# Attention scores from scaled float16 halves instead of rounded float32 halves, and a last period written out with ten products moved into the tail

## The chip, the cores and the metric

The kernel runs on one core of one Trainium2 chip. The metric is the device time of one execution in microseconds. Engine names are the profile's: PE is TensorE's matmul side and PEld its weight loads, DVE is VectorE, ACT is ScalarE, POOL is GpSimd, SP is SyncE, which only issues DMAs here. A kernel is measured several times; one of its executions is also profiled. About 0.3% (2 us) is what such a measurement can tell from no change.

## What is computed

One post-norm transformer layer on x of 4 batches x 512 tokens x 512 features, all float32. Attention has 16 query heads of 32 features and one key and value head for all of them, with rotary embedding. The feed-forward part has 1408 hidden features, with weights rounded to -1, 0, 1.

```python
q = rotary((x @ Wq + bq) as 16 heads);  k = rotary(x @ Wk + bk);  v = x @ Wv + bv
attn = softmax(q @ k.T / sqrt(32));     x = layernorm(x + (attn @ v) @ Wo + bo)
w = clip(round(w / (mean|w| + 1e-8)), -1, 1)          # for w1, w2, w3
x = layernorm(x + (sigmoid(x @ w1.T) * (x @ w2.T)) @ w3.T)
```

## The kernel before

**Periods.** The work is written out by hand for each engine, and semaphores tie the engines together. Period b (b = 0 to 3) does attention for batch b, and beside it the feed-forward part of batch b-1. Period 0 has no feed-forward work; it loads and rounds the three feed-forward weights instead (`abs_sum` on ACT, `thresholds` on DVE, `round_weight` on POOL). Periods 1 to 3 are one hardware loop, `Fori(1, B)`. A tail does the feed-forward part of batch 3 alone.

**Opening of a period.** PE projects the first four heads (q0) and k and v, multiplies the context of the batch before with Wo (`project_out`, tiles wo0 to wo3), and transposes the normed rows (`turn_h`, ht0 to ht3). DVE rotates q0 and k (`pairs`, `rotate`, `halves`), adds the residual (`attended`), computes statistics, norms, and does `h_low`. The first product of the feed-forward part, `up` of tile 0, waits for the `h_low` of ht3.

**Sixteen heads.** A head h has four score products (128 queries x 512 keys each). For each, DVE takes the row maximum (`row_max`, L702; q carries a minus sign, so it is a minimum), ACT computes the exponential with that value as bias (`exps`, L478) and sums the row, PE transposes the result (`turn`, L953), and ACT and DVE share the copies out of PSUM (`move`, L486 and L709). After each fourth head the context product follows (`context`, L1006). The list `BESIDE` says which other work stands beside head h: the up products of tile 0 to 10, the projections q2 and q3 at heads 4 and 8, and the down products dn0 to dn3 at heads 13 to 16. In period 0 q2 and q3 are projected in pieces at heads 2, 3 and 6, 7 and `halves` of q3 runs at head 9. The score tiles are a ring of three PSUM banks (four in period 0), so that a score waits for the exponential of three (four) scores before.

**Split of q and k.** The scores need more than half precision. `halves` writes the rotated q into `hi` as float32r (a rounded float32) and the remainder into `lo`; k goes to `k_st` in the same way. SP then stacks `hi`, `lo`, `hi`, `lo` of each head under each other in `q_st` with 16 small DMAs for four heads (`stack`, L283, 64 KB each, 32 partitions), and k_st holds k's parts to match, so that one product over 128 rows gives the sum of the cross products. The scale 1/sqrt(32) is put in with q's bias (L445).

**SP's order in period 0.** x transposed (`xT_sb`, two halves), the rest of Wq, the first half of w1, stack q0, rest of w1, w2, stack q1, Wo, stack q2, w3, stack q3, x into `xb` (L326), then `load_xT(1)` (L289), the next batch's transposed x. In periods 1 and 2 the next `load_xT` also stands behind stack q3.

**The tail.** PE: four `project_out`, four `turn_h`, eleven times two up tiles, four down tiles. They use the two banks `a_ps` and `b_ps` in turn. DVE norms and does `h_low` between them.

## Time and profile before

| what | us |
|---|---|
| median of 3 runs | 682.1 (681.53 to 683.32) |
| the profiled execution | 681.93, of which the traced span is 680.1 |
| PE busy in the span | 632.1 (93%) |
| DVE busy | 465.1 (68%) |
| ACT busy | 352.9 (52%) |
| POOL busy | 133.8 (20%) |

The four periods and the tail start at 0, 131.9, 286.2, 441.5 and 595.3 us on PE. Busy shares are means over stages with different limits, so that the question for each edit is which wait ends last at its place. Matmuls overlap, and a matmul's own length is longer than its share of PE's time: eight float16 products in a row last 1.90 us by their own ends, and 1.74 us from the first start to the start of what follows.

### The profile page before, as it was taken

How to read it: one execution, taken by the hardware profiler on the slowest of the kernel's cores; microseconds unless marked ns; L12 is line 12 of the kernel's file. 1: busy time of each engine (PE TensorE's matmuls, PEld its weight loads, DVE VectorE, ACT ScalarE, POOL GpSimd, SP SyncE). 2: the span in 40 equal slices, each digit the busy share in tenths (PEclk: the TensorE clock that was granted, in tenths of full speed). 3: DMA queues.
4: the chain of work that ended last, by engine and by line, in shares of the span. 5: the costliest groups of instructions: out<-in, count | busy, mean ns of one | idle time of the engine just before them, and what ended most of it. 6: DMA issues, size and time to landing. Idle time of an engine off the chain costs nothing.

```text
span 680.1 us, 10942 instructions
## 1 busy us (share of the span) xinstructions
PE 632.1 (93%) x3342; PEld 344.0 (51%) x3342; DVE 465.1 (68%) x795; ACT 352.9 (52%) x814; POOL 133.8 (20%) x148
## 2 busy tenths in 40 slices
PE   6787867899999999999999999999999999988996
PEld 2553544445656556435656555544656565543442
DVE  1767687377878976568877985567878985563333
ACT  1686696315757675114757674214757674302320
POOL 0309779231001200121000400022000400020001
PEclk9689989899999999999999999999999999998999
DMA  7670623020420220020320220020221100000001
GB/s 271 203 237 21 212 68 121 0 63 1 124 51 13 59 66 1 36 82 12 95 70 25 49 77 1 35 75 20 69 86 35 41 23 1 32 31 1 0 1 62
DMA packets 20515, 42.02 MB, mean 62 GB/s; under 512 B 4704, under 2 KB 5856, under 8 KB 19936
## 3 DMA queue, kind: packets, MB, share of 16 engines
q1 hardware_dynamic: 19488, 39.86, 19.2%
q10 hardware_dynamic: 960, 1.33, 0.5%
q8 instruction: 34, 0.56, 0.3%
q14 instruction: 33, 0.27, 0.1%
HBM read 20.20 MB, written 4.19 MB: 36 GB/s over the span
## 4 chain that ended last, share of the span: by engine, by line
PE 73%; DVE 10%; issue 7%; ACT 4%; DMA 3%; SPq 1%; POOL 1%; DVEq 0%; POOLq 0%; ACTq 0%
PE t_ps L953 14%; PE a_ps L913 11%; PE b_ps L913 11%; PE c_ps L1006 8%; PE a_ps L879 7%; PE s_ps L942 6%; PE a_ps L928 6%; PE b_ps L928 6%; DMA late<-in_w 2%; DVE sh_sb L702 2%; PE a_ps L900 2%; ACT p_sb L478 2%; SPq L283 1%; DVE stat L669 1%; PE b_ps L900 1%
## 5 line engine op out<-in xcount | busy, mean ns | idle before, releaser
L478 ACT ACTIVATE p_sb<-s_ps,sh_sb 128x512 f32<-128x512 f32 x240 | 164.2, 688 | 85.6 <-DVE sh_sb L702 85.6
L702 DVE TENSOR_REDUCE sh_sb<-s_ps 128x1 f32<-128x512 f32 x240 | 157.8, 681 | 1.5 <-PE s_ps L942 1.4
L953 PE MATMUL t_ps<-table_sb,p_sb 128*128 128x128 f32 x1024 | 140.4, 281 | 16.2 <-ACT pt_sb L486 13.9
L953 PEld LDWEIGHTS t_ps<-table_sb,p_sb 128*128 128x128 f32 x1024 | 120.6, 144 | 56.0 <-ACT p_sb L478 21.2
L709 DVE COPY pt_sb<-t_ps 128x512 f32<-128x512 f32 x128 | 88.3, 690 | 82.6 <-PE t_ps L953 80.3
L486 ACT ACTIVATE pt_sb<-t_ps 128x512 f32<-128x512 f32 x128 | 76.4, 597 | 58.1 <-PE t_ps L953 56.3
L942 PE MATMUL s_ps<-k_st,q_st 128*128 128x512 f32 x240 | 90.6, 460 | 3.7 <-DVE k_st L629 2.5
L913 PE MATMUL a_ps<-late,q 128*128 128x512 f16 x352 | 85.0, 386 | 3.5 <-DVE late L644 3.4
L913 PE MATMUL b_ps<-late,q 128*128 128x512 f16 x352 | 83.7, 381 | 0.0
L358 POOL TENSOR_TENSOR rot<-raw,table_sb 128x512 f32<-128x512 f32 x20 | 25.8, 1288 | 246.4 <-ACT raw L445 231.5
L879 PE MATMUL a_ps<-xT_sb,wq_sb 128*128 128x512 f32 x128 | 63.1, 625 | 7.9 <-DMA wq_sb<-in_wq 6.4
L382 POOL TENSOR_SCALAR rstd<-mv 128x1 f32<-128x1 f32 x32 | 8.4, 263 | 279.0 <-DVE mv L672 278.9
L1006 PE MATMUL c_ps<-pt_sb,v_sb 128*32 128x512 f32 x512 | 58.2, 595 | 0.4 <-DVE pt_sb L709 0.4
L913 PEld LDWEIGHTS a_ps<-late,q 128*128 128x128 f16 x352 | 32.0, 99 | 46.8 <-issue 7.9
L913 PEld LDWEIGHTS b_ps<-late,q 128*128 128x128 f16 x352 | 31.9, 98 | 39.5 <-issue 5.6
L942 PEld LDWEIGHTS s_ps<-k_st,q_st 128*128 128x128 f32 x240 | 42.6, 197 | 12.4 <-ACT p_sb L478 6.2
L478 ACT ACTIVATION_READ_ACCUMULATOR p_sb<-s_ps,sh_sb 128x1 f32 x240 | 48.1, 201 | 0.0
L900 PE MATMUL a_ps<-wo_sb,cx 128*128 128x512 f32 x88 | 40.2, 600 | 1.4 <-DVE late L692 1.4
L928 PE MATMUL b_ps<-q,late 128*128 128x512 f16 x176 | 41.4, 380 | 0.0
L928 PE MATMUL a_ps<-q,late 128*128 128x512 f16 x176 | 40.4, 380 | 0.0
L879 PEld LDWEIGHTS a_ps<-xT_sb,wq_sb 128*128 128x128 f32 x128 | 23.7, 198 | 32.8 <-issue 23.5
L659 DVE SCALAR_TENSOR_TENSOR b_ps<-th,b_ps 128x512 f32<-128x512 f32 x33 | 23.0, 696 | 21.5 <-PE b_ps L913 19.4
(80 smaller groups left out, 614.1 us busy)
## 6 DMA issues: line engine op xcount, KB each, us to landing
q_st<-hi SPq DMA_DIRECT2D x128, 64.0 KB, 2.0
q_st<-lo SPq DMA_DIRECT2D x128, 64.0 KB, 2.0
late<-in_w SPq DMA_DIRECT2D x2, 2816.0 KB, 11.7
xT_sb<-in_xT SPq DMA_DIRECT2D x8, 512.0 KB, 4.7
late<-in_x SPq DMA_DIRECT2D x4, 1024.0 KB, 5.6
out<-late SPq DMA_DIRECT2D x16, 256.0 KB, 2.0
late<-in_w SPq DMA_DIRECT2D x2, 1408.0 KB, 7.0
wo_sb<-in_wo SPq DMA_DIRECT2D x1, 1024.0 KB, 5.4
```

The source lines that it names most:

```text
L358: pool.tensor_tensor(rot[:, 0, :], raw[:, u % 2, :], cos_sb, ALU.mult).then_inc(cos_done, 1)
L478: act.activation(p_sb[:, h % 2, t, :], score_bank(b, n), ACT.Exp, bias=sh_sb[:, n % (2 * SR):n % (2 * SR) + 1], scale=-1.0, accum_out=sums ...
L486: act.activation(pt_sb[:, h % PTR, k, :], t_ps[k % 2][:, :], ACT.Copy).then_inc(pt_act, 1)
L702: dve.tensor_reduce(sh_sb[:, n % (2 * SR):n % (2 * SR) + 1], score_bank(b, n), AX.X, ALU.min).then_inc(maxed, 1)
L709: dve.tensor_copy(pt_sb[:, h % PTR, k, :], t_ps[k % 2][:, :]).then_inc(pt_dve, 1)
L879: mm = pe.matmul(a_ps[:, :], wq_sb[:, k, g * P:(g + 1) * P], xT_sb[:, k, :], start=(k == 0), stop=(k == DT - 1))
L900: mm = pe.matmul(ps[:, :], cx[:, g, t * P:(t + 1) * P], wo_sb[:, g, :], start=(g == 0), stop=(g == HG - 1))
L913: mm = pe.matmul(ps[:, :], w[:, k, f * P:(f + 1) * P], hT[:, s, k, :], start=(k == 0 and s == 0), stop=(k == DT - 1 and s == 1))
L928: mm = pe.matmul(ps[:, :], gT[:, s, f, t * P:(t + 1) * P], q3v[:, f, :], start=(f == 0 and s == 0), stop=(f == FT - 1 and s == 1))
L942: pe.matmul(score_bank(b, n), q_st[:, h % (QR * HPG), t * P:(t + 1) * P], k_st[:, :], start=True, stop=True).then_inc(scored, 1)
L953: mm = pe.transpose(t_ps[k % 2][:, t * P:(t + 1) * P], p_sb[:, h % 2, t, k * P:(k + 1) * P], id_sb)
L1006: mm = pe.matmul(c_ps[HD * j:HD * (j + 1), :], v_sb[:, k, :], pt_sb[:, (g * HPG + j) % PTR, k, :], start=(k == 0), stop=(k == TT - 1))
```

## The change

**Float16 halves.** `hi`, `lo`, `q_st` and `k_st` are float16. So that both halves fit into float16, q and k are multiplied by powers of two (`grow`) before they are split. The power comes from a bound of |q| and |k|: the largest |x| of each partition times the largest |w|, plus the largest |bias|, summed over the partitions by a product with ones (`add_parts` on PE), whose exponent is then taken by a bitwise and (`scales`). `shrinks` makes the inverse. The row maximum goes to `top`, and a second DVE instruction of one element a partition multiplies it with `shrink` into `sh_sb`; the exponential takes its scale from `shrink` too, where it was the constant -1.

**Where the bounds are computed.** For batch 0, at the very start for q0 and k, and at head 0 for the other heads (`REST`). For batch b+1, in period b: `x_size` of the two halves of xT behind heads 11 and 12, `bound` behind head 13, `scales` behind head 14. `shrinks` stands at the head of each period. SP waits for `x_sized` before it loads xT anew.

**Last period and tail.** The loop is now `Fori(1, B - 1)`, and period 3 is written out behind it. In period 3 the down products of dn3 stop after tile 5 (`LAST_CUT`); the ten products of tiles 6 to 10 stand in the tail, eight between ht2 and ht3 and two behind ht3. In the tail the wo and ht tiles have a PSUM bank each (`late_tile`), the norm of batch 3 is written to `xb` instead of `h_sb`, and the first up tile takes the high halves of all four k first and waits for the low ones only then.

```diff
+TOP = 11
+SIZE_AT = [11, 12]
+BOUND_AT = 13
+SCALE_AT = 14
+LAST_CUT = 6
...
-        hi = sb("hi", [P, T], F32R)
-        lo = sb("lo", [P, T], F32R)
-        q_st = sb("q_st", [P, QR * HPG, T], F32R)
-        k_st = sb("k_st", [P, T], F32R)
+        hi = sb("hi", [P, T], F16)
+        lo = sb("lo", [P, T], F16)
+        q_st = sb("q_st", [P, QR * HPG, T], F16)
+        k_st = sb("k_st", [P, T], F16)
...
                 if not last:
+                    sp.wait_ge(x_sized, (b + 1) * 2)
                     sp.wait_ge(a_filled, ain(b, "q3"))
...
-                               bias=sh_sb[:, n % (2 * SR):n % (2 * SR) + 1], scale=-1.0,
+                               bias=sh_sb[:, n % (2 * SR):n % (2 * SR) + 1],
+                               scale=shrink[:, 1, min(h // HPG, 1):min(h // HPG, 1) + 1],
...
+            def x_size(b, half):
+
+                dve.wait_ge(xT_in[half], (b + 1) * 16)
+                if half == 0:
+                    dve.wait_ge(bounded, 0 if isinstance(b, int) and b == 0 else b + 1)
+                stand(dve)
+                dve.tensor_reduce(xmax[:, half:half + 1],
+                                  xT_sb[:, half * DT // 2:(half + 1) * DT // 2, :].rearrange("p k t -> p (k t)"),
+                                  AX.X, ALU.max, apply_absolute_value=True).then_inc(x_sized, 1)
...
+            def bound(b, cols):
...
+                    dve.tensor_tensor(xmax[:, 0:1], xmax[:, 0:1], xmax[:, 1:2], ALU.max).then_inc(x_merged, 1)
...
+                dve.scalar_tensor_tensor(out=part[:, cols], in0=wmax[:, cols], scalar=xmax[:, 0:1],
+                                         in1=bmax[:, cols], op0=ALU.mult, op1=ALU.add).then_inc(bounded, 1)
...
+            def scales(b, cols, rest, ps, filled, drained, count):
...
+                dve.tensor_scalar(power[:, cols], ps[:, cols], 2.0 ** -50, 2.0 ** 60, ALU.max,
+                                  ALU.min).then_inc(drained, 1)
...
-                    dve.tensor_copy(hi[:, :], rot[:, 1, :]).then_inc(hi_done, 1)
+                    dve.tensor_scalar(hi[:, :], rot[:, 1, :], grow[:, col:col + 1], None,
+                                      ALU.mult).then_inc(hi_done, 1)
                     dve.wait_ge(hi_done, n + 1)
-                    dve.tensor_tensor(lo[:, :], rot[:, 1, :], hi[:, :].bitcast(F32),
-                                      ALU.subtract).then_inc(lo_done, 1)
+                    dve.scalar_tensor_tensor(out=lo[:, :], in0=rot[:, 1, :], scalar=grow[:, col:col + 1],
+                                             in1=hi[:, :], op0=ALU.mult, op1=ALU.subtract).then_inc(lo_done, 1)
...
                 dve.wait_ge(scored, b * H * TT + n + 1)
-                dve.tensor_reduce(sh_sb[:, n % (2 * SR):n % (2 * SR) + 1], score_bank(b, n), AX.X,
-                                  ALU.min).then_inc(maxed, 1)
+                dve.tensor_reduce(top[:, slot], score_bank(b, n), AX.X, ALU.min).then_inc(top_found, 1)
+                dve.wait_ge(top_found, b * H * TT + n + 1)
+                dve.tensor_scalar(sh_sb[:, slot], top[:, slot], shrink[:, 0, j:j + 1], None,
+                                  ALU.mult).then_inc(maxed, 1)
...
+            def next_scales(b, h):
+
+                if h in SIZE_AT:
+                    x_size(b + 1, SIZE_AT.index(h))
+                if h == BOUND_AT:
+                    bound(b + 1, EVERY)
+                if h == SCALE_AT:
+                    scales(b + 1, EVERY, 1, a_ps, a_filled, a_drained, ain(b, "next_scale"))
...
                     if h == 0:
                         pairs(b, "q1")
                         rotate(b, "q1")
+                        dve.wait_ge(wq_in, 16)
+                        w_size(2)
+                        bound(b, REST)
                     if h == 1:
+                        scales(b, REST, 1, a_ps, a_filled, a_drained, ain(b, "scale_rest"))
+                        shrinks(b, REST, 1)
                         halves(b, "q1")
+                    next_scales(b, h)
...
+                    x_size(b, 0)
+                    w_size(0)
+                    w_size(1)
+                    x_size(b, 1)
+                    bound(b, FIRST)
+                    scales(b, FIRST, 0, b_ps, b_filled, b_drained, bin_(b, "scale"))
+                    shrinks(b, FIRST, 0)
                     dve.wait_ge(table_in, 16)
+                else:
+                    shrinks(b, EVERY, 1)
...
             period(0)
-            with dve.Fori(1, B) as b:
+            with dve.Fori(1, B - 1) as b:
                 period(b)
+            period(B - 1)
...
+            def add_parts(cols, n, ps, filled, drained, count):
+
+                pe.wait_ge(bounded, n)
+                pe.wait_ge(drained, count - 1)
+                pe.matmul(ps[:, cols], ones[:, :], part[:, cols], start=True, stop=True).then_inc(filled, 1)
```

On PE, at the start of period 0, a product of `part` with ones now stands ahead of the last k tile of q0's projection, and another one between the scores of head 0 and head 1. Before:

```order
L879 MATMUL a_ps<-xT_sb,wq_sb 128x512 x4
L960 MATMUL c_ps<-xT_sb,small_sb 32x512 x4
...
L942 MATMUL s_ps<-k_st,q_st 128x512 x3
L942 MATMUL b_ps<-k_st,q_st 128x512
L942 MATMUL s_ps<-k_st,q_st 128x512 x3
L942 MATMUL b_ps<-k_st,q_st 128x512
```

and after:

```order
L1069 MATMUL a_ps<-xT_sb,wq_sb 128x512 x3
L1078 MATMUL b_ps<-part,ones 128x2
L1069 MATMUL a_ps<-xT_sb,wq_sb 128x512
...
L1150 MATMUL s_ps<-k_st,q_st 128x512 x3
L1150 MATMUL b_ps<-k_st,q_st 128x512
L1078 MATMUL a_ps<-part,ones 128x1
L1150 MATMUL s_ps<-k_st,q_st 128x512 x3
L1150 MATMUL b_ps<-k_st,q_st 128x512
```

Both products of `part` wait for DVE's `bound`, and what stands behind them on PE waits too.

On DVE, from the last copy of head 11 to the first copy of head 12 in period 0. Before:

```order
L709 COPY pt_sb<-t_ps 128x512
L588 TENSOR_REDUCE atot<-c_ps 128x1
L590 TENSOR_SCALAR thr<-atot 128x1
L593 RECIPROCAL thr<-thr 128x1
L702 TENSOR_REDUCE sh_sb<-s_ps 128x1 x2
L709 COPY pt_sb<-t_ps 128x512
```

and after:

```order
L861 COPY pt_sb<-t_ps 128x512
L675 TENSOR_REDUCE xmax<-xT_sb 128x1
L662 TENSOR_REDUCE atot<-c_ps 128x1
L664 TENSOR_SCALAR thr<-atot 128x1
L667 RECIPROCAL thr<-thr 128x1
L852 TENSOR_REDUCE top<-s_ps 128x1
L854 TENSOR_SCALAR sh_sb<-top,shrink 128x1
L852 TENSOR_REDUCE top<-s_ps 128x1
L854 TENSOR_SCALAR sh_sb<-top,shrink 128x1
L861 COPY pt_sb<-t_ps 128x512
```

The `xmax` reduction (L675) reads the next batch's xT and waits for its DMA; each row maximum has become two instructions.

On PE, the head of the tail. Before:

```order
L900 MATMUL b_ps<-wo_sb,cx 128x512 x4
L890 MATMUL a_ps<-table_sb,late 128x128 x4
L890 MATMUL b_ps<-table_sb,late 128x128 x4
L890 MATMUL a_ps<-table_sb,late 128x128 x4
L890 MATMUL b_ps<-table_sb,late 128x128 x4
L913 MATMUL a_ps<-late,q 128x512 x8
```

and after:

```order
L1099 MATMUL t_ps<-wo_sb,cx 128x512 x4
L1087 MATMUL t_ps<-table_sb,late 128x128 x4
L1087 MATMUL c_ps<-table_sb,late 128x128 x4
L1087 MATMUL s_ps<-table_sb,late 128x128 x4
L1136 MATMUL b_ps<-q,late 128x512 x8
L1087 MATMUL s_ps<-table_sb,late 128x128 x4
L1136 MATMUL b_ps<-q,late 128x512 x2
L1116 MATMUL a_ps<-late,q 128x512 x8
```

The ten products of dn3 (`b_ps<-q,late`) come from behind heads 15 and 16 and the context product of period 3.

## Rows read from the trace of the kernel before

**Rows 1.** The page's head: span; engine, busy us (share) x instructions
```profile
span 680.1 us, 10942 instructions
PE 632.1 (93%) x3342; PEld 344.0 (51%) x3342; DVE 465.1 (68%) x795; ACT 352.9 (52%) x814; POOL 133.8 (20%) x148
```

**Rows 2.** Windows by stage: window length, busy PE, PEld, DVE, ACT, POOL; clock, DMA
```profile
0.00:22.50 22.50, 13.62 (x42) 5.49 (x42) 8.38 (x14) 4.74 (x7) 4.26 (x9) 0.98 0.65 227
22.50:131.90 109.40, 85.34 (x486) 53.88 (x486) 73.67 (x129) 80.90 (x190) 66.25 (x48) 0.89 0.39 130
131.90:160.80 28.90, 27.97 (x98) 12.64 (x95) 20.28 (x40) 7.17 (x14) 6.13 (x11) 1.00 0.15 37
160.80:286.20 125.40, 124.74 (x741) 70.92 (x741) 94.75 (x157) 76.62 (x184) 12.01 (x13) 1.00 0.17 48
286.20:315.90 29.70, 28.04 (x93) 12.54 (x93) 21.24 (x42) 7.12 (x14) 6.85 (x13) 1.00 0.20 55
```

**Rows 3.** Chain of work, period 1, head 11: start us, us on the chain, what
```profile
236.06 0.70 PE s_ps L942 x3
236.76 1.74 PE a_ps L913 x8
238.51 0.87 PE t_ps L953 x8
239.38 0.24 PE s_ps L942
```

**Rows 4.** Timeline of DVE, period 0, heads 11 and 12: start, us, what, [idle before]
```profile
99.78 0.69 DVE L709 COPY pt_sb<-t_ps 128x512 f32<-128x512 f32 x1 [0.84 <-PE t_ps L953]
...
100.57 0.15 DVE L590 TENSOR_SCALAR thr<-atot 128x1 f32<-128x1 f32 x1
100.76 0.16 DVE L593 RECIPROCAL thr<-thr 128x1 f32<-128x1 f32 x1
100.84 1.27 DVE L702 TENSOR_REDUCE sh_sb<-s_ps 128x1 f32<-128x512 f32 x2
```

**Rows 5.** Timeline of all engines, period 1, from head 11 to head 12
```profile
239.42 0.69 DVE L709 COPY pt_sb<-t_ps 128x512 f32<-128x512 f32 x1 [0.23 <-PE t_ps L953]
...
241.48 0.23 ACT L478 ACTIVATION_READ_ACCUMULATOR p_sb<-s_ps,sh_sb 128x1 f32 x1
241.48 0.70 DVE L659 SCALAR_TENSOR_TENSOR b_ps<-th,b_ps 128x512 f32<-128x512 f32 x1 [0.78 <-PE b_ps L913]
```

**Rows 6.** Timeline of PE, period 1, head 12
```profile
241.99 0.94 PE L942 MATMUL s_ps<-k_st,q_st 128*128 128x512 f32 x3
```

**Rows 7.** Timeline of SP's DMA issues, period 0, heads 9 to 12
```profile
88.45 1.14 SPq L283 DMA_DIRECT2D q_st<-hi  x2
...
100.20 0.69 SPq L326 DMA_DIRECT2D late<-in_x  x1
101.01 0.90 SPq L289 DMA_DIRECT2D xT_sb<-in_xT  x2
```

**Rows 8.** The xT tile between 100 and 104 us: time from issue to landing
```profile
DMA to landing us min/median/max: 6.3/6.8/7.2
```

**Rows 9.** Timeline of all engines, period 0, start and heads 0 to 2
```profile
6.42 6.13 PE L879 MATMUL a_ps<-xT_sb,wq_sb 128*128 128x512 f32 x8 [6.42 <-DMA wq_sb<-in_wq]
...
8.07 0.21 ACT L572 ACTIVATE small_sb<-small_sb 128x4 f32<-128x4 f32 x1 [3.83 <-DMA small_sb<-in_small]
...
13.53 0.75 DVE L605 STREAM_SHUFFLE rot<-raw 128x512 f32<-128x512 f32 x1
...
24.91 2.13 PE L942 MATMUL s_ps<-k_st,q_st 128*128 128x512 f32 x3 [0.32 <-ACT p_sb L478]
```

**Rows 10.** Timeline of ACT, period 0, head 2
```profile
41.48 1.38 ACT L495 ACTIVATE q<-late 128x1408 f16<-128x1408 f32 x1 [1.81 <-DMA late<-in_w]
```

**Rows 11.** Timeline of PE, head of the tail
```profile
615.31 3.43 PE L913 MATMUL a_ps<-late,q 128*128 128x512 f16 x8 [1.42 <-DVE late L644]
```

**Rows 12.** Windows, first up products of the tail: columns as in rows 2
```profile
616.00:620.00 4.00, 4.00 (x13) 1.52 (x12) 0.00 (x0) 0.60 (x1) 0.00 (x0) 0.64 0.00 0
```

274 lines of the change are left out of this document (207 added, 67 removed).

## The prediction, as it was put on record

> **What bounds the kernel now.** I read the busy table first [rows 1]: PE is busy 93% of the span, DVE 68%. That mean hides two regimes, so I cut the span into stages [rows 2]. In the heads of period 1 (160.8 to 286.2 us) PE is busy 124.7 of 125.4 us: PE is the bound, and only shorter products or a new wait move the time. DVE has 94.8 of 125.4 us there, 76%. In the heads of period 0 (22.5 to 131.9 us) PE is busy 85 of 109 us, ACT 81 and DVE 74: no engine is full, and the loop score, row maximum, exponential, transpose, copy sets the pace, so that any latency put into it counts. Before 22.5 us everything waits for the first loads and the first q and k. An opening of a later period (131.9 to 160.8) has PE at 27.97 of 28.90 us. In the tail PE waits for DVE's last `h_low` and then runs slowly [rows 11, 12].
>
> **Cheaper scores.** The chain of a head gives three scores 0.70 us, the fourth 0.24, eight float16 products 1.74 [rows 3]. A float16 product with 512 columns takes 1.74/8 = 0.217 us, so four scores fall from 0.94 to 0.87: 0.07 to 0.08 us a head. Over the 48 heads of periods 1 to 3 that is **-3.6 us**. The float32r score is already nearly as fast as a float16 one; that leaves little to win. The stacked DMAs have half the bytes; their issue, about 0.63 us each (16 from 88.45 to 100.1), is what SP pays [rows 7], and I take it as unchanged.
>
> **The second instruction of each row maximum.** Two independent reductions of 0.68 us take 1.27 us, so one follows the other after 0.59 [rows 4]. The dependent pair L590, L593 shows the price of a small operation that waits for the one before it: 0.15 us long, the next one starts 0.19 after it, and after the last one the independent reduction starts 0.08 later [rows 4]. A reduction and its multiply so take 0.68 + 0.04 + 0.08 = 0.80 instead of 0.59: **+0.2 us of DVE**, and of latency, 256 times. VectorE: DVE Perf Modes, section "The DRAIN you can't avoid", in the Trainium skill, says that a semaphore between two DVE operations costs nothing beside the flush; the trace disagrees, since an independent successor starts before its predecessor's end and a dependent one 0.04 us after it. By that rule the pair would cost only the multiply's 0.08, which is a rival below.
>
> In period 0's loop about twelve row maxima of the heads 3 to 16 lie on the path (an estimate, one for most heads): **+2.4**. In periods 1 to 3 a head with an up product lasts 0.70+1.74+0.87+0.24+1.74+0.87 = 6.2 us [rows 3]. DVE idles 0.23 + 0.78 = 1.0 us of it [rows 5]; four multiplies with a register wait each take 0.8 to 1.0. So DVE is then full, but just holds. The score that waits for the last exponential of head 11 (third of the 0.94 us from 241.99, so about 242.5) follows the end of it at 241.71 by 0.8 us [rows 5, 6]; the exponential comes 0.5 later. Steady heads lose nothing. Where DVE already has `halves` beside (heads 1 to 4, 5, 9), it does. I take 1.5 us in each of periods 1 and 2 and 0.9 in period 3, **+3.9**, from 0 to 9. In the three openings one row maximum stands ahead of an `attended`, and `shrinks` ahead of q0: 0.4 each, **+1.2**. That the exponential reads its scale from memory I take as free, since its bias already comes from there.
>
> **The start.** DVE needs wq, small and the scaled bias (8.07 + 0.21 = 8.3 us) [rows 9]. Then come 1024 elements of x, 512 and 128 of weights, and 1024 of x again: at 0.59 per 512 [rows 4] about 3.1 us, and four small steps, 0.7: `bound` ends near 12.1. PE has three of four k tiles done at 6.42 + 0.75 x 6.1 = 11.0 to 11.5, waits, and does the rest: q0 comes about 1 us later, and the shuffle of 13.53 near 14.7. **+1.2**, from 0.5 to 3; the q0 stack and the big weight loads behind it follow.
>
> **Head 0 of period 0.** Behind the row maxima of head 0, DVE now sizes 1536 elements of Wq (1.8 us) and PE's product behind it holds back the scores of head 1, which stood at 24.91 [rows 9], until about 29.6. I follow that through ACT's two `abs_sum` there: ACT is 3.4 us late at head 2, and had a wait of 1.81 for w2 to spare [rows 10]. **+1.6**, from 0 to 4.
>
> **The wait for xT.** This is the term that decides. In period 0, `x_size(1)` stands behind DVE's last copy of head 11, over at 100.4 us [rows 4]. It needs xT of batch 1, which SP issues at 101.01, behind all of stack q3 and x; it lands 6.3 to 7.2 us later, near 107.7 [rows 7, 8]. Both times hang on the same `halves` of q3 (SP's stack starts at 88.45), so a later start of both changes nothing; DVE's own path to 100.4 gets perhaps 0.8 longer by the multiplies. DVE then stands still 6 to 6.5 us; behind it are queued the third threshold, the row maxima of head 12 and the copy of head 11, for which ACT and PE wait. The reduction takes 1.2. I give 0.5 back, since ACT waited then anyway: **+7.0**, from 4 to 9. Nothing later in period 0 makes it up, since the loop has no slack; POOL's rounding of w3, which follows that threshold, is not needed before period 1's feed-forward part.
>
> In periods 1 and 2 the same issue order lets xT land at about the end of head 11 (PE is slower there, DVE later); no wait, but 2 x 1.2 us on a full DVE against 0.8 us of spare time: **+2.0** together. `bound`, `scales` and the product `add_parts`: **+1.8** over three periods. PE's idle stretch in period 0 may bring the half clock for a while, as the mean of 0.89 there shows it now [rows 2]: **+0.5**.
>
> **The written-out period.** The opening of period 2, behind a jump back, lasts 29.70 us, that of period 1 28.90 [rows 2]; with PE's own short gap at the jump, period 3 can gain **-1.4**, at most 2.
>
> **The tail.** Ten products leave the PE-bound part: **-2.2**, as 10 x 0.217. They fill the 3 us in which PE waited for norms. The up tile now needs only high halves at first: the wait of 1.42 [rows 11] shrinks by about **-0.5**. Its eight products took 3.43 us instead of 1.74, at the lower clock (0.64 mean in that window: the granted clock was 1.2 GHz for part of it) after PE had been mostly idle [rows 11, 12]. With PE busier just before, I take that back: **-1.7**, from 0.
>
> **The sum.** -3.6+2.4+3.9+1.2+1.2+1.6+7.0+2.0+1.8+0.5-1.4-2.2-0.5-1.7 = **+12.2 us**, on a profiled execution of 681.9 (span 680.1, median 682.1, nearly the same): **694**.
>
> **Rivals.**
> *DMA issue falls with the bytes.* If a stack of 32 KB pieces is issued in 7 us instead of 11.7, xT lands 4 us earlier, and DVE waits 2 us. 7.0 becomes 3: 690. For it: the issue of 128 rows of xT takes only 0.45 us each (0.90 for two). Against: an issue of 1 MB costs 0.69 and one of 64 KB 0.6, so bytes hardly matter [rows 7]. 0.17.
> *DVE falls behind in the heads.* Here it becomes the bound of periods 1 and 2: if a multiply costs 0.3 with its register waits, 1.2 a head meet 1.0 of idle time, 0.2 us over some 20 heads and more at q heads: 3.9 becomes 11 and 2.0 becomes 4: 703. 0.15.
> *Faster.* The place is head 11 of period 0, the mechanism that xT is on the chip before DVE asks for it. Then 7.0 is the reduction's 1.2 alone, and everything that DVE gets more in period 0 can hide where ACT waits anyway. That gives 12.2 - 5.8 = 6.4 us at my other prices, still slower; it ends faster only with the multiplies at 0.08 (6.3 becomes 2.5, the page's rule again), and the 2.0, the 1.6 and half of the 1.8 and the 1.2 of the start hidden: 6.4 - 3.8 - 2.0 - 1.6 - 0.9 - 0.6 = -2.5, or 679. It decides when the stack of q3 ends over 6 us sooner than it does [rows 7], for which no row speaks. 0.05.
> *No change.* The same with one of these costs left: 680 to 684. 0.04.
> *The forecast,* 691 to 699: 0.59.
>
> By these cases faster by over 0.3% (2 us, what a measurement can tell) has 0.05, the same 0.04, slower 0.91. The range for 8 in 10 is 685 to 705: the bounds of the xT wait and of the full DVE, and with them the first two rivals.
>
> **What would show it.** Right: DVE idle 5 us or more before the `xmax` reduction of head 11 in period 0, released by a DMA of xT; PE's period 1 starting 12 to 15 us later than 131.9; its heads in period 1 with PE idle under 4 us; eight first up products of the tail in under 2.2 us; scores of 0.22 us each. Wrong: xT landing before DVE needs it; idle PE all through the heads of periods 1 and 2, with DVE as releaser; the half clock still there in the tail.

## The result: 720 us, three times the loss that was forecast

The kernel before ran in 682.0 us (median of this comparison), the changed one in 720.0 us (717.8 to 723.7): a ratio of 1.057, 95% interval 1.052 to 1.061. The forecast was 694 us with a range of 685 to 705: the direction was right, the size was not, +38 us instead of +12.

The head of the page of the changed kernel, and two of its groups (line, engine, operation, names, shapes, count | busy us, mean ns | idle before):

```profile
span 717.2 us, 10991 instructions
PE 635.4 (89%) x3352; PEld 329.5 (46%) x3352; DVE 538.1 (75%) x1099; ACT 378.9 (53%) x814; POOL 133.8 (19%) x148
...
L550 ACT ACTIVATE p_sb<-s_ps,sh_sb,shrink 128x512 f32<-128x512 f32 x240 | 186.9, 780 | 118.2 <-DVE sh_sb L854 117.6
...
L854 DVE TENSOR_SCALAR sh_sb<-top,shrink 128x1 f32<-128x1 f32 x256 | 54.8, 214 | 9.1
```

Against [rows 1] PE has almost the same busy time, DVE 73 us more and ACT 26 more: 54.8 of DVE's are the new multiplies, and each exponential takes longer. ACT now stands 118 us in wait of a bias, where it stood 86. The windows of the changed kernel, cut where the same instructions stand as in [rows 2] (columns as there):

```profile
0.00:23.70 23.70, 14.10 (x44) 5.47 (x44) 12.82 (x26) 4.74 (x7) 4.57 (x9) 1.00 0.56 204
23.70:152.50 128.80, 85.34 (x491) 49.60 (x491) 95.79 (x209) 87.56 (x190) 65.95 (x48) 0.85 0.27 96
152.50:181.40 28.90, 27.75 (x96) 12.16 (x92) 20.77 (x41) 6.34 (x12) 6.09 (x10) 1.00 0.07 19
181.40:312.90 131.50, 126.22 (x747) 68.05 (x746) 110.50 (x227) 84.00 (x186) 12.14 (x13) 1.00 0.11 33
312.90:346.90 34.00, 29.82 (x92) 12.54 (x92) 22.44 (x44) 6.34 (x12) 6.53 (x12) 0.95 0.10 33
```

Start +1.2 us. Heads of period 0: 128.8 instead of 109.4, **+19.4**, with the same work on PE and DVE 22 us busier. Heads of period 1: 131.5 instead of 125.4, +6.1; PE is idle 5.3 us there. The last line is a surprise of its own: the opening of period 2 takes 34.0 us, 5.1 more than that of period 1, and in the kernel before it was 29.70 against 28.90.

The granted clock of TensorE moves with the time as well. The four runs of the changed kernel took 717.8, 719.3, 720.7 and 723.7 us at mean granted clocks of 0.973, 0.970, 0.967 and 0.961; the runs of the kernel before mostly show 0.978. In period 0 of the profiled executions, from key product to key product, 1.2 GHz was granted for 37.5 us, against 23.9 in the kernel before. A wait of PE and the lower clock come together here, and no run separates them: how much of the +19.4 us is the clock's stays open.

Kernels of this study can be laid beside each other by PE's first key product of each period. The table does it for eleven of them and gives the time from one to the next, worked out from one profiled execution each ("period 3" runs to the last product of the tail; the start moves by a microsecond or two with the first DMAs):

| kernel | start | period 0 | period 1 | period 2 | period 3 and tail |
|---|---|---|---|---|---|
| before | 12.5 | 123.1 | 154.3 | 155.3 | 229.0 |
| changed | 13.7 | 142.4 | 160.4 | 164.5 | 230.1 |
| no multiply (a_no_mult) | 14.6 | 135.9 | 156.1 | 155.2 | 225.3 |
| neither (a_neither) | 13.9 | 135.8 | 155.5 | 154.2 | 224.8 |
| no later sizes (a_no_next) | 13.6 | 135.8 | 159.0 | 158.0 | 230.1 |
| 24 instructions shifted (a_shift) | 13.6 | 143.0 | 160.9 | 160.4 | 230.1 |
| changed, loop written out (a_unrolled) | 13.7 | 146.3 | 159.4 | 159.4 | 230.2 |
| no scales at all (plain_f16_tail) | 11.5 | 119.2 | 153.9 | 152.3 | 224.5 |
| the same, written out (plain_unrolled) | 11.4 | 120.9 | 152.3 | 152.2 | 224.5 |
| before + multiply (b_mult) | 13.0 | 130.5 | 158.2 | 158.5 | 232.7 |
| before + idle multiply (b_mult_free) | 11.7 | 124.7 | 155.0 | 155.3 | 229.7 |

### The profile page after: what moved, and what is told of

Its sections match the earlier page's. It is cut to its first block, busy times and chain, and to the rows that moved or that the text cites. A ratio compares the mean times of both kernels' runs of the same rounds, so it can differ in the third digit from the quotient of the medians.

```text
span 717.2 us, 10991 instructions
## 1 busy us (share of the span) xinstructions
PE 635.4 (89%) x3352; PEld 329.5 (46%) x3352; DVE 538.1 (75%) x1099; ACT 378.9 (53%) x814; POOL 133.8 (19%) x148
## 4 chain that ended last, share of the span: by engine, by line
PE 48%; DVE 28%; issue 12%; ACT 7%; DMA 2%; POOL 1%; SPq 1%; DVEq 1%; ACTq 0%; POOLq 0%
PE t_ps L1161 10%; DVE top L852 8%; PE c_ps L1214 7%; PE a_ps L1136 5%; PE b_ps L1136 5%; PE b_ps L1121 5%; PE a_ps L1121 5%; PE a_ps L1069 4%; ACT p_sb L550 3%; PE s_ps L1150 3%; DVE pt_sb L861 3%; DVE sh_sb L854 2%; ACT pt_sb L559 2%; DVE late L805 2%; PE a_ps L1099 2%
## 5 line engine op out<-in xcount | busy, mean ns | idle before, releaser
L550 ACT ACTIVATE p_sb<-s_ps,sh_sb,shrink 128x512 f32<-128x512 f32 x240 | 186.9, 780 | 118.2 <-DVE sh_sb L854 117.6
L852 DVE TENSOR_REDUCE top<-s_ps 128x1 f32<-128x512 f32 x240 | 163.3, 680 | 2.7 <-PE s_ps L1150 2.6
L559 ACT ACTIVATE pt_sb<-t_ps 128x512 f32<-128x512 f32 x128 | 76.2, 595 | 37.6 <-PE t_ps L1161 37.6
L1150 PE MATMUL s_ps<-k_st,q_st 128*128 128x512 f16 x240 | 77.8, 401 | 9.1 <-ACT p_sb L550 6.3
L1121 PE MATMUL a_ps<-late,q 128*128 128x512 f16 x344 | 81.3, 379 | 2.5 <-DVE late L785 2.0
L854 DVE TENSOR_SCALAR sh_sb<-top,shrink 128x1 f32<-128x1 f32 x256 | 54.8, 214 | 9.1
L1121 PEld LDWEIGHTS b_ps<-late,q 128*128 128x128 f16 x352 | 34.4, 98 | 38.0
L550 ACT ACTIVATION_READ_ACCUMULATOR p_sb<-s_ps,sh_sb,shrink 128x1 f32 x240 | 47.1, 196 | 0.0
L1150 PEld LDWEIGHTS s_ps<-k_st,q_st 128*128 128x128 f16 x240 | 24.5, 105 | 30.5 <-ACT p_sb L550 21.4
L1099 PE MATMUL a_ps<-wo_sb,cx 128*128 128x512 f32 x72 | 34.8, 628 | 2.1 <-DVE late L839 2.1
```

What stands on the lines that cost most here:

```text
L550: act.activation(p_sb[:, h % 2, t, :], score_bank(b, n), ACT.Exp, bias=sh_sb[:, n % (2 * SR):n % (2 * SR) + 1], scale=shrink[:, 1, min(h / ...
L559: act.activation(pt_sb[:, h % PTR, k, :], t_ps[k % 2][:, :], ACT.Copy).then_inc(pt_act, 1)
L852: dve.tensor_reduce(top[:, slot], score_bank(b, n), AX.X, ALU.min).then_inc(top_found, 1)
L854: dve.tensor_scalar(sh_sb[:, slot], top[:, slot], shrink[:, 0, j:j + 1], None, ALU.mult).then_inc(maxed, 1)
L1099: mm = pe.matmul(ps[:, :], cx[:, g, t * P:(t + 1) * P], wo_sb[:, g, :], start=(g == 0), stop=(g == HG - 1))
L1121: mm = pe.matmul(ps[:, :], w[:, k, f * P:(f + 1) * P], hT[:, s, k, :], start=(k == 0 and s == 0), stop=(k == DT - 1 and s == 1))
```

## The experiments

Times are medians, ratios are against the kernel before on the same chip with the 95% interval. The kernel before has medians of 679.9 to 682.0 us in these comparisons, so that a difference between kernels of two comparisons carries 1 to 2 us of that. The steps of 2.6 to 5.5 us that single edits take off the changed kernel, and the last steps from a_no_mult to a_neither and from plain_f16_tail to plain_unrolled, have overlapping intervals; there the trace has to speak too.

### Taking the two prices out of the changed kernel

**a_const_exp.** In `exps` of the changed kernel:

```
-  scale=shrink[:, 1, min(h // HPG, 1):min(h // HPG, 1) + 1],
+  scale=-2.0 ** -11,
```

> The changed kernel with one edit: the exponential takes its scale as the constant -2^-11 (the value that these inputs give in every batch) instead of reading it from the tile shrink. Theory A: the 92 ns that each exponential has become longer (780 instead of 688) lie on the path in period 0, where ACT is one of three engines in a loop without slack, and partly later, since the last score of a head and the transposes wait for the last exponential. 64 exponentials of period 0 by 0.09, half to all on the path, are 3 to 6 us; a third of the 192 others 4 to 6: 720 falls to 708 to 713, ratio to the kernel before 1.040 to 1.046. Rival (my prediction): the scale from memory is free in effect, since ACT is busy half of the span only: 718 to 720.

Measured: 716.6 us, 1.052 (1.049 to 1.055), 3.3 us less than the changed kernel. (The constant is not the factor of every batch after all, so the edit leaves out the right scale there; the work is the same.) The scale from memory seems not to be free, but theory A had put it too high. The intervals overlap; b_exp_scale below settles it.

**a_no_mult.** In `row_max`, with `TOP = 6` instead of 11, so that the factor left out is 1/2:

```
-  dve.tensor_reduce(top[:, slot], score_bank(b, n), AX.X, ALU.min).then_inc(top_found, 1)
-  dve.wait_ge(top_found, b * H * TT + n + 1)
-  dve.tensor_scalar(sh_sb[:, slot], top[:, slot], shrink[:, 0, j:j + 1], None,
-                    ALU.mult).then_inc(maxed, 1)
+  dve.tensor_reduce(sh_sb[:, slot], score_bank(b, n), AX.X, ALU.min).then_inc(maxed, 1)
```

> The changed kernel with the multiply behind each row maximum left out: the minimum is written straight into the tile of the biases. (TOP is 6 instead of 11, so that the factor that is left out is 1/2 here; the bias is then another shift of the same row, which the softmax cancels.) Theory A: a pair of reduction and multiply takes 0.85 instead of 0.60, 0.25 us of DVE and of latency 256 times; this is the largest part of the 38 us: 17 to 24 us less, 696 to 703. Rival B (the sizes of my prediction, 0.2 on the path for 12 maxima, 3.9 in the later heads, 1.2 in the openings): 7.5 us less, 712.

Measured: 694.5 us, 1.020 (1.017 to 1.023). **25.4 us hang on the multiply**, two thirds of the whole loss, and just above theory A's range. By the table 6.5 lie in period 0, 4.3 in period 1, 9.3 in period 2, 4.8 in period 3. The 9.3 hold a second thing: with the multiplies gone, DVE's stop at the loop's jump is 3.55 us and not 5.84, and the opening of period 2, from the first key product to the first transpose of the heads, is 32.3 us and not 37.6, where the opening of period 1 loses 0.7. Some 4.5 us of the 25.4 so belong to the second stop at the jump (below), and about 21 to the multiplies themselves.

**a_neither.** Both edits together, with `TOP = 6` and -0.5 as the scale (again not the factor of every batch).

> The changed kernel without the multiply and with a constant scale (-1/2) of the exponential; the sizes of x and the weights, bound, scales and their waits all stay. Theory A: what is left over the kernel before is the wait for xT, head 0, the start and the sizes, against the gains of scores and tail: 686 to 693, and the two prices nearly add up. Rival C: one of the two hides the other (whichever engine is the later sets the pace), so that this is no lower than the better of the two single kernels by more than 2 us.

Measured: 691.9 us, 1.016 (1.013 to 1.019), 28.1 us less than the changed kernel. 25.4 + 3.3 = 28.7: the prices add up, and rival C, which allowed 2 us below the better single one, falls with 2.7 only narrowly and within the noise. What is left over the kernel before sits in period 0.

### The parts that were to gain

**plain_f16_tail.** The changed kernel with `x_size`, `w_size`, `bound`, `add_parts`, `scales`, `shrinks`, their waits and their uses of the banks deleted, and plain copies in `halves`:

```
-  dve.tensor_scalar(hi[:, :], rot[:, 1, :], grow[:, col:col + 1], None, ALU.mult)
+  dve.tensor_copy(hi[:, :], rot[:, 1, :])
```

> The changed kernel with everything that belongs to the scales taken out: float16 halves of q and k as they are (factor 1), a constant -1 in the exponential, no multiply behind the row maximum, no sizes, bound, scales, shrinks; the tail and the written-out last period stay. Theory A: with both price items gone a kernel was still 10 us above the kernel before, and its period 0 held 12.7 us of that, its later periods nothing: sizes and their waits in period 0 are that rest, and the gains of score and tail are real: 673 to 677, faster than the kernel before by 5 to 8 us. Rival: the rest lies in the float16 halves or their DMAs themselves (smaller packets), then it stays above 682.

Measured: 670.3 us, 0.985 (0.981 to 0.988): **faster than the kernel before by 10.8 us**, more than was expected. So 691.9 - 670.3 = **21.6 us are the price of finding the scales** and putting them into the halves, by the table 2.4 at the start, 16.6 in period 0, 1.6 and 1.9 in periods 1 and 2.

**tail_only.** The same with `hi`, `lo`, `q_st`, `k_st` in float32r.

> As before it, but with q and k in float32r as in the kernel before: only the written-out last period, the ten moved products, the other banks of the tail and the high halves first. My prediction had -1.4 -2.2 -0.5 -1.7 = -5.8 for these, 676. Theory A, after the trace of the changed kernel (the stretch behind the last context product fell from 79.6 to 76.8 us, the openings hardly changed): 677.5 to 679.5. Rival: no gain in the median (681 to 683), since the ten products only move the wait.

Measured: 677.2 us, 0.993 (0.991 to 0.996): 3.9 us gained, by the interval 3 to 6.

**b_f16.** In the kernel before:

```
-  hi = sb("hi", [P, T], F32R)      (and lo, q_st, k_st)
+  hi = sb("hi", [P, T], F16)
```

> The kernel before with one edit: hi, lo, q_st and k_st are float16 instead of float32r (factor 1, constant scale). My prediction: 0.07 to 0.08 us a head in 48 heads, -3.6: 678.4. Theory A, from the trace of the changed kernel (weight loads of the scores 105 instead of 197 ns): 677 to 679. Rival: PE waits elsewhere for what it gains, 681 to 682.

Measured: 675.3 us, 0.992 (0.988 to 0.995): 5.8 us gained, by the interval 4 to 8. Groups of this kernel: the exponential with its constant scale, the score's product (392 ns, in the kernel before 460) and its weight load (100 ns, before 197):

```profile
L478 ACT ACTIVATE p_sb<-s_ps,sh_sb 128x512 f32<-128x512 f32 x240 | 164.3, 688 | 83.6 <-DVE sh_sb L702 83.5
L942 PE MATMUL s_ps<-k_st,q_st 128*128 128x512 f16 x240 | 74.3, 392 | 4.5 <-DVE k_st L629 2.5 <-ACT p_sb L478 1.7
...
L942 PEld LDWEIGHTS s_ps<-k_st,q_st 128*128 128x128 f16 x240 | 23.7, 100 | 19.4 <-ACT p_sb L478 8.4 <-issue 3.5
```

### Putting the two prices on the kernel before

**b_mult.**

```
-  dve.tensor_reduce(sh_sb[:, ...], score_bank(b, n), AX.X, ALU.min).then_inc(maxed, 1)
+  dve.tensor_reduce(top[:, slot], score_bank(b, n), AX.X, ALU.min).then_inc(top_found, 1)
+  dve.wait_ge(top_found, b * H * TT + n + 1)
+  dve.tensor_scalar(sh_sb[:, slot], top[:, slot], ones[:, 0:1], None, ALU.mult).then_inc(maxed, 1)
```

> The kernel before with one edit: the minimum of each score row goes to a tile of its own and a second instruction multiplies it by 1.0, read from a tile, into the tile of the biases; nothing else. Theory A: the multiply costs by itself what it costs in the changed kernel (25 us there): 702 to 710; of this, DVE's jump back to the start of the loop body costs about 2 us more than before at each of the two returns, since with 64 more instructions in the body the trace of the changed kernel shows DVE idle for issue 5.84 us there and 3.55 without the multiplies. Rival B (my prediction's sizes): 0.2 us on twelve maxima, 3.9, 1.2: 689.5. Rival E: the multiply hurts only together with the sizes on a full DVE: 685 to 692.

Measured: 700.7 us, 1.029 (1.026 to 1.032), **19.7 us for the multiply alone**. Just under theory A, far from rivals B and E. The part on the jump back was wrong: it was as cheap as before here. By the table: 7.4 in period 0, 3.9, 3.2 and 3.7 in the later ones.

**b_mult_free.**

```
+  dve.tensor_scalar(spare[:, n:n + 1], ones[:, 1:2], ones[:, 0:1], None,
+                    ALU.mult).then_inc(spare_set, 1)      (behind the old reduction)
```

(In the later periods it also waits for the idle multiply of 32 before it in `spare_set`, long done.)

> The kernel before with one more instruction behind each of the 256 reductions of the row maxima: a multiply of the same size (128x1, factor from a tile) that reads constants and writes to a tile that nobody reads. The reduction writes the bias itself, so no exponential waits for the multiply, and the multiply does not wait for the reduction. Theory O (DVE's time as such, half of the 0.25 us being the wait of the dependent one and half the multiply): 689 to 693. Theory L (only what stands between a score and its exponential counts): 681 to 684.

Measured: 685.9 us, 1.008 (1.005 to 1.010): 5.0 us, between the two theories. The idle multiply costs a quarter of the 19.7; the rest, 14.7, comes with the dependence: both the longer pair on DVE and the later bias. First the timeline of DVE with the idle multiply (a reduction, the multiply, the next reduction), then that of b_mult:

```profile
63.58 0.68 DVE L705 TENSOR_REDUCE sh_sb<-s_ps 128x1 f32<-128x512 f32 x1
64.19 0.20 DVE L708 TENSOR_SCALAR spare<-ones 128x1 f32<-128x1 f32 x1
64.31 0.67 DVE L705 TENSOR_REDUCE sh_sb<-s_ps 128x1 f32<-128x512 f32 x1
```

```profile
65.80 0.68 DVE L705 TENSOR_REDUCE top<-s_ps 128x1 f32<-128x512 f32 x1
66.51 0.21 DVE L707 TENSOR_SCALAR sh_sb<-top,ones 128x1 f32<-128x1 f32 x1
66.64 0.68 DVE L714 COPY pt_sb<-t_ps 128x512 f32<-128x512 f32 x1
```

With the idle multiply the next piece of work starts 0.73 us after the reduction, with the dependent one 0.84, without any 0.59 to 0.60. And the exponential waits for 65.80 + 0.71 + 0.21 = 0.92 us from the reduction's start instead of 0.68.

**b_exp_scale.**

```
-  bias=sh_sb[:, n % (2 * SR):n % (2 * SR) + 1], scale=-1.0,
+  bias=sh_sb[:, n % (2 * SR):n % (2 * SR) + 1], scale=minus[:, :],
```

> The kernel before with one edit: the exponential reads its scale, -1, from a tile of one column instead of having it as a constant. Theory A: 0.09 us on each of the 64 exponentials of period 0, where no engine has slack, and little later: 683 to 686. Rival (my prediction): free, 680.5 to 682. Rival H: the last exponential of a head holds up PE in every period, 64 times 0.09, so that 5.5 to 6 us come on top: 687.

Measured: 685.0 us, 1.006 (1.004 to 1.009): +4.1, theory A. Its exponential:

```profile
L480 ACT ACTIVATE p_sb<-s_ps,sh_sb,minus 128x512 f32<-128x512 f32 x240 | 186.2, 779 | 75.5 <-DVE sh_sb L706 75.5
```

779 ns instead of 688 with the constant. The trace so gives 91 ns for one more operand from memory, beside the bias that comes from there already. The Trainium skill has the rule that was missed ("ScalarE: Activation LUTs", section "What ACT_TABLE_LOAD costs"): each [128,1] operand read through a pointer adds about 93 ns to the instruction. The trace agrees.

### Where the scales cost

**a_size_later.** `SIZE_AT = [12, 13]` instead of `[11, 12]`.

> The changed kernel with the two reductions over the next batch's xT behind the heads 12 and 13 instead of 11 and 12, nothing else. The trace shows DVE idle 4.9 us before the first of them in period 0, released by the DMA of xT. Theory A (the term of 7.0 in my prediction): 4 to 6 us go, 714 to 716. Rival D: the wait covers time that PE and ACT lose anyway in this loop, or the heads 12 and 13 lose it instead (the copy of head 12 waits behind the reduction as that of head 11 did): under 2 us, 718 to 720.

Measured: 717.4 us, 1.053 (1.050 to 1.056): 2.6 us, between the theories. In the profiled execution the step from head 11 to 12 is 9.8 us instead of 16.4, but the way from head 12 to period 1 takes 3.5 us longer: part of the wait only moved on.

**a_xT_first.** In SP's `period`:

```
+  if not last: (wait for x_sized and q3, then) load_xT(b + 1)
   sp.wait_ge(scored, (b * H + 2 * HPG) * TT)
   stack(b, 3)
-  if not last: ... load_xT(b + 1)
```

> The changed kernel with one thing moved: SP issues the next batch's xT ahead of the stack of q3 instead of behind it (it then waits for q3's projection only), so that it has landed before DVE asks for it behind head 11 of period 0. Theory A: the 4.94 us in which DVE stood for that DMA go, the two reductions of 1.2 us stay: 714 to 716. Rival D: another wait takes its place (as when the reductions came one head later, which gave 2.6 of the 4.9), 717 to 719.

Measured: 714.4 us (712.4 to 718.3), 1.052 (1.047 to 1.056): 5.5 us, theory A; the step from head 11 to 12 is 10.9 us instead of 16.4. The place in the changed kernel, timeline of DVE and then of SP:

```profile
109.70 0.69 DVE L861 COPY pt_sb<-t_ps 128x512 f32<-128x512 f32 x1 [2.33 <-PE t_ps L1161]
115.33 1.22 DVE L675 TENSOR_REDUCE xmax<-xT_sb 128x1 f32<-128x1024 f32 x1 [4.94 <-DMA xT_sb<-in_xT]
```

```profile
96.60 1.14 SPq L349 DMA_DIRECT2D q_st<-hi  x2
...
108.85 0.89 SPq L355 DMA_DIRECT2D xT_sb<-in_xT  x2
```

and the same place with the load moved, where the reduction starts straight behind the copy:

```profile
108.53 0.69 DVE L861 COPY pt_sb<-t_ps 128x512 f32<-128x512 f32 x1 [0.34 <-PE t_ps L1161]
109.14 1.21 DVE L675 TENSOR_REDUCE xmax<-xT_sb 128x1 f32<-128x1024 f32 x1
```

**a_no_next.** `next_scales`, the `add_parts` of head 14 and `shrinks` of the later periods deleted; batch 0's factors serve for all.

> The changed kernel without the sizes of the later batches: no reduction over xT, no bound, add_parts and scales behind the heads 11 to 14, no shrinks in the openings; the factors of batch 0 serve for all batches. Start, head 0, the multiply and the scale from memory stay. Theory A: the traces of the kernel without both price items and of the plain one differ by 7.8 us from head 11 to 12 of period 0, by 5.5 us from head 12 to the next period and by 1.6 to 1.9 us in each of the periods 1 and 2, 17 us in all: 720 falls to 701 to 705. Rival (the sizes of my prediction: 7.0 + 2.0 + 1.8 + 0.4): 708 to 710.

Measured: 703.5 us, 1.034 (1.031 to 1.036), 16.4 us less than the changed kernel: theory A. 4 to 5 of these are the jump, below, which is cheap in this kernel (3.33 us idle; opening of period 2 32.6 us), so that 11 to 12 are left for the sizes of the later batches.

### The jump back to the start of the loop

**a_unrolled.** `for b in range(1, B - 1)` in place of `Fori` on all five engines.

> The changed kernel with the loop over the periods 1 and 2 written out on all five engines; the same work in the same order, no jump back. In the trace of the changed kernel the opening of period 2, behind the jump back, is 5.1 us longer than that of period 1 (37.6 against 32.5 us from the first key product to the first transpose); DVE stands 5.84 us for issue there, against 3.3 to 3.8 at the jump of the kernels with fewer instructions. Theory F: the multiply makes the jump back dearer, by a load of instructions: 713 to 716. Rival G: the straight program has the same load to make, only elsewhere, 718 to 720.

Measured: 715.3 us, 1.050 (1.047 to 1.053): 4.7 us, theory F on the time. In the profiled execution periods 1 and 2 are 1.0 and 5.1 us shorter, but period 0 is 3.9 longer, with 1.2 GHz granted for 54.6 us of it instead of 37.5.

**b_mult_pad.** b_mult with `stand(dve)` behind the two `move` calls of each head in `heads`.

> The kernel before with the multiply (700.7 us alone, 457 recorded instructions of DVE per pass of the loop) and 32 more instructions in DVE's loop body that only add to a semaphore which nobody reads, one behind each copy of a transposed block: 489 per pass. Theory F (the number of instructions in the body makes the jump back dear): DVE stands 5.3 us or more for issue at both jumps, against 3.34 and 3.65, and the time is 704 to 712. Rival (what the changed kernel does first behind its jump, the shrinks, makes it dear): the idle stretch stays under 4 us, 700 to 703.

Measured: 699.8 us, 1.027 (1.023 to 1.031), no more than b_mult. So more instructions in the body, on which theory F rested, did not bring the second stop.

**a_shift.**

```
+  for _ in range(24):
+      stand(dve)
   period(0)
```

> The changed kernel with 24 instructions ahead of everything that DVE does (each only adds to a semaphore that nobody reads; DVE waits for the first DMA there anyway). The loop body is the same, but starts 24 instructions later in DVE's stream. Theory P (position decides): the second stop of 2.1 us behind the jump goes, the idle stretch ahead of the shrinks is 3.3 to 3.8 instead of 5.84 us, the opening of period 2 is as long as that of period 1 (32.5 us), and the time is 715 to 717. Rival: what the body does there decides, nothing changes, 719 to 721.

Measured: 715.8 us, 1.052 (1.048 to 1.055), **4.1 us less for 24 instructions more**: theory P. In the table period 2 is 4.1 us shorter, and no other period is. DVE's first operation behind the jump, in the changed kernel, in a_shift, and (its first jump) in b_mult_pad:

```profile
321.51 0.23 DVE L725 TENSOR_SCALAR shrink<-power 128x2 f32<-128x2 f32 x1 [5.84 <-issue]
```

```profile
320.06 0.23 DVE L725 TENSOR_SCALAR shrink<-power 128x2 f32<-128x2 f32 x1 [3.68 <-issue]
```

```profile
302.79 0.01 DVE L607 LOAD_MASK_SELECT rot<-raw  x1 [3.49 <-issue]
```

Each jump stops DVE for about 3 us at the branch: in the changed kernel its sequencer branches at 315.8 and does its next work at 319.2. There a second stop of 2.1 us follows, three instructions on (319.4 to 321.5), with nothing to wait for; moved by 24 places it is gone, and the opening of period 2, counted from the first key product to the first transpose of the heads, is 33.1 us instead of 37.6. The 4.5 us are more than the stop. PE was busy for 18.7 of the 22.6 us up to 335.5, and then the changed kernel has a stretch at the lower clock, 1.2 GHz, which the four kernels with the second stop show in this opening and none of the others; its window (clock third from the end):

```profile
335.50:339.00 3.50, 3.50 (x5) 1.33 (x4) 2.81 (x6) 0.00 (x0) 0.79 (x2) 0.51 0.07 19
```

"Runtime: NRT & Kernel Launch" in the Trainium skill, section "Instruction fetch mechanics", says that instructions are fetched in blocks and that a taken branch out of the blocks at hand has to wait for the fetch of its target. That fits both stops, if a border of blocks lies just behind the loop's start; where such borders lie no run here shows.

### Versions made of what was learned

**plain_unrolled.** plain_f16_tail with the loop written out.

> The plain kernel (float16 halves as they are, the new tail, no scales) with the loop written out. There DVE stands 3.6 us for issue at the jump, but PE reaches the first transpose of the heads in 31.2 us either way, and only the 1.5 us between the last head and the first key product (13.9 against 12.4) can go: 668 to 670 from 670.3. It is also the version that ought to beat all others. Rival G: nothing or slightly slower, 670 to 672.

Measured: **668.0 us, 0.982 (0.980 to 0.984)**, the fastest kernel of the study, 12 us under the kernel before. Like plain_f16_tail it leaves out the powers of two, so it holds only where q and k and their remainders fit into float16 as they are.

**a_first_unrolled.** a_xT_first with the loop written out.

> The changed kernel with both edits that gave something: xT issued ahead of the stack of q3 (714.4 alone) and the loop written out (715.2 alone). If the two terms are separate, 5.5 and 4.7 us add up: 708 to 711. If they overlap, 713 to 715.

Measured: 709.3 us, 1.042 (1.040 to 1.045): 10.7 us, against 5.5 + 4.7; the two terms are separate.

## Why the prediction had the sign and not the size

Its sum beside what the runs gave, in us:

| part | forecast | measured |
|---|---|---|
| float16 scores | -3.6 | -5.8 (b_f16) |
| tail and written-out period | -5.8 | -3.9 (tail_only); together with the scores -10.8 |
| second instruction of each row maximum | +7.5 | +25.4 in the changed kernel, some 4.5 of it the second stop at the jump; 19.7 alone |
| scale of the exponential from memory | 0 | +3.3, 4.1 alone |
| start, head 0, xT, sizes, bounds, clock | +14.1 | +21.6 |
| sum | +12.2 | -10.8 + 21.6 + 28.1 = +38.9, beside +38.0 |

The last row agrees by construction: its three numbers are the distances from the kernel before to plain_f16_tail, on to a_neither and on to the changed kernel (28.1 is the last one; 25.4 and 3.3 are the two prices one at a time). The sign was not luck: with the multiplies and the scale left out, the search for the scales alone (21.6) outweighs the gains (10.8), as the forecast had it with 14.1 against 9.4.

**The row maxima: the step that failed.** "In period 0's loop about twelve row maxima of the heads 3 to 16 lie on the path (an estimate, one for most heads)" is the sentence. No row stood behind one for each head. I had the cost of one pair right to 0.05 us (0.80, measured 0.84), and then laid it on 12 of the 64 maxima of period 0, where I had just written that no engine is full and any latency counts. Alone it costs 7.4 us there, over 64 maxima 0.12 each: about half of the 0.25 of every pair, not all of it for every fifth. (The 7.4 are net of 2.6 us that the step from head 2 to head 3 gives back, see the gains below; without that step it is 10.) "Steady heads lose nothing" failed as well. It rested on DVE's idle time of 1.0 us a head against 0.8 to 1.0 more work. In these heads DVE does fit, but with no idle time left it is always late. The timeline of DVE in a head of period 1, where in [rows 5] there stood waits of 0.23 and 0.78 for PE:

```profile
201.61 0.21 DVE L854 TENSOR_SCALAR sh_sb<-top,shrink 128x1 f32<-128x1 f32 x1
201.74 0.68 DVE L805 TENSOR_TENSOR late<-b_ps,late 128x512 f16<-128x512 f32 x1
202.34 0.68 DVE L852 TENSOR_REDUCE top<-s_ps 128x1 f32<-128x512 f32 x1
203.05 0.21 DVE L854 TENSOR_SCALAR sh_sb<-top,shrink 128x1 f32<-128x1 f32 x1
203.19 0.68 DVE L852 TENSOR_REDUCE top<-s_ps 128x1 f32<-128x512 f32 x1
203.90 0.21 DVE L854 TENSOR_SCALAR sh_sb<-top,shrink 128x1 f32<-128x1 f32 x1
204.03 0.68 DVE L861 COPY pt_sb<-t_ps 128x512 f32<-128x512 f32 x1
```

Each piece follows the last at once. PE meanwhile stands for ACT, which stands for DVE, as here shortly before. First an exponential of ACT that waits for DVE, then PE, which waits for the copy that stands behind such exponentials in ACT's order:

```profile
196.90 0.78 ACT L550 ACTIVATE p_sb<-s_ps,sh_sb,shrink 128x512 f32<-128x512 f32 x1 [0.57 <-DVE sh_sb L854]
```

```profile
199.16 1.09 PE L1161 MATMUL t_ps<-table_sb,p_sb 128*128 128x128 f32 x8 [0.66 <-ACT pt_sb L559]
200.09 0.81 PE L1150 MATMUL s_ps<-k_st,q_st 128*128 128x512 f16 x3
```

From the first transpose of head 0 to that of head 15 period 1 takes 114.5 us with the multiply and 110.5 without, 4.0 in each of three periods, where the term had 1.5, 1.5 and 0.9. The openings lose 0.7 and 0.9 us where no jump stands ahead of them, twice the 0.4 each of the forecast. The rival that DVE falls behind named this mechanism with 703 us; it too left period 0 at 2.4.

**The jump.** 4.1 to 4.7 us of the loss belong to no operation of the change. The written-out period was priced from the two openings of [rows 2] as if a jump's cost were a constant of the kernel. It hangs on where the loop's start falls in DVE's stream, as a_shift shows. This could not be read from the kernel before. An ordinary jump came out near the forecast: in plain_f16_tail the way from head 15 to the next key product is 13.9 us with the jump in it and 12.4 with the period written out, 1.5 against the 1.4 of the term.

**The exponential.** "I take as free, since its bias already comes from there" was an argument by likeness, with no row, and on an engine that is part of period 0's loop. 91 ns on 256 exponentials, 23 us of ACT's time, gave 3.3 to 4.1 us.

**The wait for xT: right.** The term was +7.0. The stack of q3 and xT moved together, as said: 96.60 against 88.45, 108.85 against 101.01 [rows 7]. DVE stood 4.94 us instead of the 6 to 6.5, since its own path from the `halves` of q3 to the last copy of head 11 had grown by 2.5 us (95.43 to 110.39, before 87.97 to 100.47) and not by 0.8. From head 11 to 12 a_neither takes 8.0 us more than plain_f16_tail, and moving the load gives back 5.5. The rival that the issue falls with the bytes is out: the 16 issues of the stack take 11.5 us with half the bytes and 11.6 before. (11.6 / 16 is 0.73 us each; the prediction's 0.63 is a slip, on which no term rests.)

**Bound and scales: too low in period 0.** 1.8 us were given for all three periods; in a_neither period 0 alone loses 5.4 us from head 12 on against plain_f16_tail, with one reduction over xT (1.2) among them. Timeline of DVE and then POOL in the changed kernel:

```profile
132.45 0.66 DVE L693 TENSOR_TENSOR xmax<-xmax 128x1 f32<-128x1 f32 x1
133.28 1.27 DVE L697 SCALAR_TENSOR_TENSOR part<-wmax,xmax,bmax 128x3 f32<-128x3 f32 x1 [0.18 <-DVE xmax L693]
```

```profile
131.74 1.36 POOL L440 TENSOR_SCALAR late<-late 128x1408 f32<-128x1408 f32 x1
133.18 1.37 POOL L442 TENSOR_SCALAR q<-late 128x1408 f16<-128x1408 f32 x1
```

Each of DVE's tiny operations ends where POOL's rounding beside it ends: 132.45 + 0.66 = 133.11 and 131.74 + 1.36 = 133.10; 133.28 + 1.27 = 134.55 = 133.18 + 1.37. With POOL idle the same operation takes 0.22 us, in period 1 of the same kernel:

```profile
287.44 0.22 DVE L697 SCALAR_TENSOR_TENSOR part<-wmax,xmax,bmax 128x3 f32<-128x3 f32 x1 [0.19 <-DVE xmax L693]
```

and so does that of the start, with 128x2 elements:

```profile
12.16 0.22 DVE L697 SCALAR_TENSOR_TENSOR part<-wmax,xmax,bmax 128x2 f32<-128x2 f32 x1 [0.19 <-DVE xmax L693]
...
14.77 0.73 DVE L740 STREAM_SHUFFLE rot<-raw 128x512 f32<-128x512 f32 x1
```

The delay of xT is not needed for this: in a_xT_first POOL's rounding of w3 starts at 110.9 and not at 117.1, and the two operations still take 1.05 and 1.27. That the rounding "is not needed before period 1's feed-forward part" was true and beside the point. In a_neither four such operations lose 3.6 us together; that these lie on the path is argued, since no run takes POOL's rounding away from beside them. "GPSIMD Engine Reference" in the Trainium skill, section "1. Specifications", says that POOL shares its interfaces to SBUF with DVE, and that DVE's instructions contend for them when they have two inputs from SBUF or run in a performance mode with two ports. Both operations here have two such inputs, and the trace agrees. The copy of L870, with one input, was held too (1.39 us at 120.33 beside POOL, 0.43 without); whether it ran in such a mode no row shows.

**Start and head 0.** The shuffle was put near 14.7 and came at 14.77, +1.24 (second row above). At head 0 I followed the delay through ACT and found 1.6 left; a_neither's first transpose, counted from the first key product, is 4.5 us behind plain_f16_tail's, and 3.2 of that are still there at head 11. Timeline of PE there; the first score of head 1 stood at 24.91 [rows 9] and was put at 29.6:

```profile
31.46 0.58 PE L1078 MATMUL a_ps<-part,ones 128*128 128x1 f32 x2 [6.39 <-DVE part L697]
...
31.91 1.44 PE L1150 MATMUL s_ps<-k_st,q_st 128*128 128x512 f16 x3
```

**The gains.** The eight first up products of the tail were to come in under 2.2 us with the clock back; in [rows 11, 12] they took 3.43 at 0.64. Now, timeline and window (clock third from the end):

```profile
653.82 2.07 PE L1116 MATMUL a_ps<-late,q 128*128 128x512 f16 x8 [0.35 <-ACT late L522]
```

```profile
652.00:656.00 4.00, 3.25 (x16) 1.45 (x17) 2.40 (x5) 0.66 (x2) 0.07 (x1) 1.00 0.00 0
```

Right, yet tail and written-out period gave 3.9 and not 5.8, which lies just inside the interval; from the last context product to the last product it is 76.8 us instead of 79.6. The scores gave more than 3.6: 1.0 us in the heads of each later period as said (108.7 instead of 109.7), and more in period 0, to which the term gave nothing: 3.8 us in b_f16. Most of that is one step, from head 2 to head 3, where ACT waits for w2 [rows 10]. It takes 8.6 us in the kernel before, 9.1 in tail_only and 8.4 in b_mult_free, where ACT stands 1.81, 2.14 and 1.52 us for w2; in all other kernels that wait is under 0.7 and the step 5.1 to 6.0. The wait shrinks when w2 comes sooner (12.5 us after its issue in b_f16, 14.0 before) and also when ACT itself comes later, as in b_mult and b_exp_scale; so the slower kernels hide part of their price there.

By the list of what would show it: the wait for xT (4.94 us, against 5 or more), the tail and the scores came out right or nearly so; PE's period 1 starts 20.6 us later and not 12 to 15, and PE idles 5.3 us in period 1's heads and not under 4. The first is the latency that was priced too low in period 0, where DVE is busy 96 of 129 us; the second is the sign of the full DVE.
